# A layernorm-and-adapter kernel on one core: a fourth rotating PSUM bank, two biases folded into the transposed state, the residual fetched again by DMA, and a new order on every engine

## The reference

```
xn = layernorm(x)
# attention branch
q = elu(split(xn @ Wq + bq)) + 1 ;  k = elu(split(xn @ Wk + bk)) + 1 ;  v = split(xn @ Wv + bv)
k = k / sqrt(sum(k*k, per head) + 1e-6)
out = merge((q k^T) v) @ Wo + bo
y = xn + out ;  att = (y - mean(y)) / sqrt(var(y) + 1e-6) * gamma + beta
# feed-forward branch, blk = 0, 1, 2 ; linear_l(a) = a @ dequant(q_l)^T + bias_l + (a @ la_l^T) @ lb_l^T
h = xn
for blk in range(3):
    t = gelu(layernorm(linear_{2 blk}(h)) * ln_gamma[blk] + ln_beta[blk])
    h = linear_{2 blk + 1}(t) + h
result = x + att + h
```

## Time and profile before

| | |
|---|---|
| time, median of 3 runs | 634.25 us (634.12 to 634.41) |
| the profiled execution's own time | 636.37 us |
| its span, first to last instruction | 634.6 us |
| mean granted TensorE clock | 0.983 of 2.4 GHz |
| PE busy | 602.0 us, 95% |
| DVE, ACT, POOL busy | 498.5, 446.8, 414.2 us (79%, 70%, 65%) |
| one body (batches 1 to 6) | 74.8 to 74.9 us |

### The profile page before, as it was taken

The page is one execution under the profiler, slowest core; times in us unless marked ns, Lnnn a source line. Parts: engine busy times, 40 slices in busy tenths (PEclk is TensorE's granted clock), DMA queues, the critical chain, the costliest instruction groups (busy, mean ns, idle before and its releaser), DMA issues.

```text
span 634.6 us, 10275 instructions
## 1 busy us (share of the span) xinstructions
PE 602.0 (95%) x3357; PEld 515.6 (81%) x3357; DVE 498.5 (79%) x1079; ACT 446.8 (70%) x699; POOL 414.2 (65%) x361
## 2 busy tenths in 40 slices
PE   7999999899998999989998999989999899989996
PEld 6888879788887888878787888878888787877875
DVE  2678689787888869788797868887787886978578
ACT  2558876858678586786778776784967857777653
POOL 3766766676476756757477674867667585765664
PEclk9999999899998999989999999989999899999999
DMA  8201001200021000300002000120002000010001
GB/s 239 71 3 34 33 1 41 93 1 2 1 99 33 0 0 0 132 0 0 0 33 99 0 0 0 71 61 0 0 0 106 26 0 0 0 67 1 1 1 67
DMA packets 9442, 20.88 MB, mean 33 GB/s; under 512 B 2367, under 2 KB 4302, under 8 KB 9422
## 3 DMA queue, kind: packets, MB, share of 16 engines
q1 hardware_dynamic: 8944, 20.22, 9.5%
q10 hardware_dynamic: 478, 0.41, 0.2%
HBM read 12.24 MB, written 8.39 MB: 33 GB/s over the span
## 4 chain that ended last, share of the span: by engine, by line
PE 51%; DVE 16%; ACT 12%; POOL 10%; issue 7%; DMA 2%; DVEq 0%; POOLq 0%; ACTq 0%; SPq 0%
PE bank L1427 14%; PE bank L1554 9%; PE bank L1433 7%; PE bank L1565 6%; PE bank L1527 3%; POOL sqs L404 3%; ACT fw L614 2%; POOL XNB L399 2%; DMA out_dram<-RES 2%; DVE Y L1030 2%; PE bank L1606 2%; DVE RES L1036 2%; POOL rsf L368 2%; DVE Y L1010 2%; PE bank L1519 2%
## 5 line engine op out<-in xcount | busy, mean ns | idle before, releaser
L253 POOL TENSOR_TENSOR gl<-fw,gh 128x512 fp32r<-128x512 f32 x80 | 102.6, 1298 | 55.9 <-ACT gh L619 55.8
L404 POOL TENSOR_TENSOR sqs<-fw 128x512 f32<-128x512 f32 x48 | 61.8, 1287 | 51.0 <-ACT fw L604 50.8
L604 ACT ACTIVATE fw<-bank,b1c 128x512 f32<-128x512 f32 x96 | 61.6, 683 | 46.4 <-PE bank L1433 46.2
L614 ACT ACTIVATE fw<-fw,vec 128x512 f32<-128x512 f32 x96 | 74.9, 808 | 9.7 <-DVE fw L935 9.4
L935 DVE SCALAR_TENSOR_TENSOR fw<-bank,b1c,rb 128x512 f32<-128x512 f32 x96 | 68.2, 744 | 10.7 <-ACT rb L610 10.7
L368 POOL TENSOR_TENSOR rsf<-vef,neghalf 128x4 f32<-128x4 f32 x48 | 51.6, 1074 | 33.8 <-DVE vef L928 31.3
L258 POOL TENSOR_TENSOR hTl<-hT,hTh 128x512 fp32r<-128x512 f32 x40 | 57.9, 1468 | 16.4 <-ACT hTh L623 16.3
L1554 PE MATMUL bank<-K,XN 128*128 128x256 f32 x256 | 61.9, 379 | 0.0
L610 ACT ACTIVATE rb<-bank 128x512 f32<-128x512 f32 x48 | 28.6, 595 | 45.3 <-PE bank L1527 45.3
L1598 PE MATMUL bank<-M,qT 128*128 128x256 f32 x256 | 59.4, 379 | 0.0
L368 POOL TENSOR_TENSOR rs<-ve,neghalf 128x2 f32<-128x2 f32 (+1 forms) x48 | 39.7, 835 | 29.9 <-DVE ve L1021 18.5
(11 more groups left out here) (148 smaller groups left out, 1681.1 us busy)
## 6 DMA issues: line engine op xcount, KB each, us to landing
X<-in_L_attn_x_dram SPq DMA_DIRECT2D x16, 512.0 KB, 3.7
out_dram<-RES SPq DMA_DIRECT2D x14, 512.0 KB, 2.6
XNB<-in_L_ffn_qweights_dram SPq DMA_DIRECT2D x2, 512.0 KB, 7.4
out_dram<-RES SPq DMA_DIRECT2D x4, 256.0 KB, 2.1
RES<-in_L_ffn_qweights_dram SPq DMA_DIRECT2D x1, 512.0 KB, 6.3
Y<-in_L_ffn_lora_a_dram ACTq DMA_DIRECT2D x4, 96.0 KB, 7.6
Wp<-in_L_attn_Wq_dram SPq DMA_DIRECT2D x1, 256.0 KB, 4.9
Wp<-in_L_attn_Wk_dram SPq DMA_DIRECT2D x1, 256.0 KB, 5.2
```

The lines of the kernel that those rows point to most:

```text
L253: engine.tensor_tensor(gl[:, h, m, :], fw[:, h, m, :], gh[:, h, m, :].bitcast(F32), ALU.subtract).then_inc(g_low[h][m], 1)
L404: pool.tensor_tensor(sqs[:, h, :], fw[:, h, 0, :], fw[:, h, 1, :], ALU.add).then_inc(sqs_ready[h], 1)
L604: act.activation(fw[:, h, m, :], FB[h][m][:], ACT.Square, bias=b1c[:, m, j:j + 1]).then_inc(sq_ready[h], 1)
L614: act.activation(fw[:, h, m, :], fw[:, h, m, :], ACT.Gelu, bias=lnb[:, m, j:j + 1], scale=lng[:, m, j:j + 1]).then_inc(g_ready[h], 1)
```

## The change

**Banks.** `AB` joins as a fourth rotating bank, but with a list of its own: the uses in `ON_SIDE` take it in turn (`SIDE`), the others rotate over the three (`RING`). G is one of its uses. **Residual.** `RES` is filled by a second DMA of x (`load_res` on SP, after the store of the batch before); `base_x`, `beta_sum` and two broadcast rows go. Beta plus the last bias is added, once for all batches, to the bias of block 1's second linear, so that the state hT carries it from there; what block 2's first linear would make of it is subtracted from its bias (`bias_last`, `shift_sums`, `bias_shift`, once in the head). **Variance.** The row sums stay in the bank and the step that scales them and adds epsilon reads them there. **`base_xn`** works by pairs of tiles: four of 128x512 a batch in place of two of 128x1024. **Orders.** All queues are written in a new order.

```
-                pool.tensor_tensor(RES[:, h * HT:(h + 1) * HT, :], X[:, h * HT:(h + 1) * HT, :],
-                                   beta_r[:].unsqueeze(1).broadcast_to([P, HT, D]), ALU.add).then_inc(x_based, 1)
+            def base_xn(i, p, at):
+                pool.tensor_tensor(XNB[:, 2 * p:2 * p + 2, :], XN[:, 2 * p:2 * p + 2, :],
+                                   bo_r[:].unsqueeze(1).broadcast_to([P, 2, D]), ALU.add).then_inc(xn_based, 1)
...
+            def load_res(i, h, at):
+                    sp.wait_ge(stored[h], 16 * i)
+                sp.dma_start(RES[:, h * HT:(h + 1) * HT, :],
+                             x_rows[bass.ds(i, 1), :, h * HT:(h + 1) * HT, :].rearrange("o p t d -> (o p) t d")
+                             ).then_inc(res_loaded[h], 16)
...
-                sp.wait_ge(x_based, nth(i, 2, h))
+                sp.wait_ge(xn_ready, nth(i, NT, h * HT + HT - 1))
                 load_x(i + 1, h)
...
-                dve.tensor_reduce(vsum[:, h, :], RB[r][:].rearrange("p (t n) -> p t n", t=HT), AX_X, ALU.add
+                dve.tensor_reduce(RB[r][:, 0:HT], RB[r][:].rearrange("p (t n) -> p t n", t=HT), AX_X, ALU.add
-                dve.tensor_scalar(vef[:, h, :], vsum[:, h, :], 1.0 / D, EPS_LN, ALU.mult, ALU.add
+                dve.tensor_scalar(vef[:, h, :], RB[r][:, 0:HT], 1.0 / D, EPS_LN, ALU.mult, ALU.add
...
+ON_SIDE = {("k", 1), ("k", 3), ("rs", 1, 0), ("g",), ("m",), ("out", 1), ("out", 3),
+           ("w", 1), ("w", 3), ("w", 5), ("sumv",), ("xt0", 0, 1)}
+                lists, banks = (SIDE, 1) if use in ON_SIDE else (RING, NROT)
...
# PE, body
                 turn_squares(i, 1, 0, BODY)
+                project_q(i, 0, 1, BODY)
                 spread_rstd(i, 1, 0, BODY)
                 project_q(i, 0, 0, BODY)
-                project_q(i, 0, 1, BODY)
                 project_q(i, 1, 0, BODY)
# ACT, body
                 g_higher(i, 0, 2, 0)
+                ln1_normalise(i + 1, 1, BODY)
+                rb_copy(i, 1, 2, BODY)
                 g_higher(i, 0, 2, 1)
-                rb_copy(i, 1, 2, BODY)
```

More of the change, by code:

```diff
@@ L27 @@
 NEWTON = 3
+NVEC = 2 * NBLK + 2 * NBLK + 1
 HEAD, BODY, TAIL = range(3)
@@ L220, in block_kernel @@
         xT_ready = sem("xT_ready")
-        rot_full = [sem(f"rot_full{n}") for n in range(NROT)]
+        rot_full = [sem(f"rot_full{n}") for n in range(NROT + 1)]
         ffn_full = [[sem(f"ffn_full{h}{m}") for m in range(NC)] for h in range(2)]
@@ L320, in body @@
             def body(i):
+                load_res(i, 0, BODY)
+                load_res(i, 1, BODY)
                 next_x(i, 0)
@@ L326, in tail @@
             def tail(i):
+                load_res(i, 0, TAIL)
+                load_res(i, 1, TAIL)
                 store_pair(i, 0)
@@ L462, in head @@
                 ffn_root(0, 0, 1)
+                ln1_root(1, 0)
                 ffn_root(0, 1, 1)
-                base_x(0, 1, HEAD)
+                base_xn(0, 3, HEAD)
                 g_lower(pool, 0, 0, 1, 1)
-                base_xn(0, 1, HEAD)
                 g_lower(pool, 0, 1, 1, 0)
@@ L1126, in bias_centre, with bias_last, bias_shift @@
                 ins.then_inc(vecs_ready, 1)
+            def bias_last():
+                dve.wait_ge(vecs_ready, 2)
+                dve.tensor_tensor(shift[:], vec[:, :, NVEC - 1], vec[:, :, NL - 1], ALU.add).then_inc(shift_ready, 1)
+                dve.wait_ge(shift_ready, 1)
+                dve.tensor_tensor(vec[:, :, NL - 3], vec[:, :, NL - 3], shift[:], ALU.add).then_inc(shift_ready, 1)
+                dve.tensor_copy(shiftr[:, :, 0], shift[:]).then_inc(shift_split, 1)
+                dve.wait_ge(shift_split, 1)
+                dve.tensor_tensor(shiftr[:, :, 1], shift[:], shiftr[:, :, 0].bitcast(F32), ALU.subtract
+                                  ).then_inc(shift_split, 1)
+            def bias_shift():
+                r, n = rotating(0, ("shift",), HEAD)
+                dve.wait_ge(vecs_ready, 3)
+                dve.wait_ge(rot_full[r], n + 1)
+                for part in range(2):
+                    if part:
+                        dve.wait_ge(shift_out, 1)
+                    dve.tensor_tensor(b1c[:, :, NBLK - 1], b1c[:, :, NBLK - 1],
+                                      RB[r][:, 0:2 * NC].rearrange("p (c two) -> p c two", two=2)[:, :, part],
+                                      ALU.subtract).then_inc(shift_out, 1)
             def bias_first():
@@ L1550, in add_g @@
                     pe.wait_ge(kh_ready, nth(i, NT // 2, t // 2))
-                if t == 0 and at != HEAD:
-                    pe.wait_ge(g_copied, nth(i - 1, 1, 0))
+                if t == 0:
+                    take(i, ("g",), at)
                 for c in range(NC):
@@ L1645, in row_sums, with shift_sums @@
                         ins = pe.matmul(RB[r][:, 2 * m:2 * m + 2], w[:, 0, k, m * P:(m + 1) * P], onesr[:],
+                                        start=(n == 0), stop=(n == len(pairs) - 1))
+                ins.then_inc(rot_full[r], 1)
+            def shift_sums():
+                r = take(0, ("shift",), HEAD)
+                pe.wait_ge(wT_split, NL - 1)
+                pe.wait_ge(shift_split, 2)
+                pairs = [(k, w) for k in range(NC) for w in (WTl, WTh)]
+                for m in range(NC):
+                    for n, (k, w) in enumerate(pairs):
+                        ins = pe.matmul(RB[r][:, 2 * m:2 * m + 2], w[:, NL - 2, k, m * P:(m + 1) * P], shiftr[:, k, :],
                                         start=(n == 0), stop=(n == len(pairs) - 1))
@@ L1869, in tail @@
                 spread_rstd(i, 0, 0, TAIL)
-                project_k(i, 2, TAIL)
                 project_k(i, 3, TAIL)
                 turn_squares(i, 1, 0, TAIL)
+                project_q(i, 0, 0, TAIL)
                 spread_rstd(i, 1, 0, TAIL)
+                second_high(i, 0, 0, TAIL)
+                second_low(i, 0, 0)
+                project_q(i, 1, 0, TAIL)
+                second_high(i, 1, 0, TAIL)
                 project_q(i, 0, 1, TAIL)
-                second_high(i, 0, 0, TAIL)
```

527 lines of the change are left out of this document (264 added, 263 removed), and 27 rows, old and new, of tables (BODY_USES, HEAD_USES, TAIL_USES).

## The result

627.23 us, median of 4 runs (627.18 to 627.6), against 634.18 (633.34 to 634.41) for the kernel before in the same session: a ratio of 0.9894 [0.9877, 0.9911], 7.0 us faster. The forecast was 622.4, 11.8 us faster. The profiled execution took 627.22 us, span 625.5, against 636.37 (span 634.6), so that the two profiles differ by 9.15 us. In a later session the medians were 627.04 us and 636.25, 9.2 us apart: how large the gain comes out depends on which of its times the kernel before shows (see the experiments).

A forecast was written before the change was run, and what follows sets the result against it. PE bounds the kernel, with a stall at spread_rstd and the lower clock behind it costing 3.9 us a body. Bodies 8.4, head 2.2 and tail 1.2 sum to 11.8 us off 634.25: 622.4 us, range 608 to 634.5.

The forecast's parts named there:

- bodies: Six bodies: each gains 1.4 us, 8.4 us in all.
- head: Before body 1: two project_q replace two pairs of fillers; between 0 and -4 us, taken as -2.2.
- tail: After the bodies: same stall, same 1.39 us filling, partly given back; between +1 and -3 us, taken as -1.2.
- The stall: PE at spread_rstd of half 1, block 0: one project_q in front cuts idleness from 2.3 to about 1.0 us.
- Most of that would fall into waits anyway: If the lower clock stayed behind the stall, most of its 1.6 us a body would fall into waits.
- No stall as short as 1.04 us brings the clock down in the tail, and not even the one of 2.18 us does: From the tail's stalls: full clock taken behind the shortened stall in the bodies.
- ACT late next: Second products of block 0: PE waits 0.8 and 0.7 us for copies of g; of 3.0 us, 1.5 are left.
- DVE after that: Residual of half 1 to block 1's variance: 7.8 to 8.35 us for 7.04; gain at spread_rstd taken as 1.2.
- The rest of a body: Block 1's spread_rstd to body's end: no change to squares of block 2; 0.2 us of remaining idleness given the new order.
- Cut loop, added DMA, variance in the bank: base_x off the path once the loop is cut, 1 MB a batch of DMA hidden, bank read taken as nothing.
- The fourth bank: PE's banks: each reader comes before its bank is wanted, closest at spread_rstd of half 1, 14.0 against 15.0.
- Slower rival: ACT's ln1_normalise ahead of the last rb_copy delays the last block, up to 3.3 us a body: 642; chance 0.16.

The follow-up runs named there:

- after_unfill: Changed kernel with project_q (0, 1) put back behind spread_rstd (1, 0) in the body: 631.09 us, against 627.04 for the changed kernel.
- before_cut: Kernel before with RES filled by DMA and no base_x, beta and last bias left out of the sum: 636.14 us, ratio 1.0004 to before.
- before_fill_cut: Kernel before with both project_q (0, 0) moved in front of spread_rstd (1, 0) and RES by DMA without base_x: 638.66 us, ratio 1.005 to before.
- after_end: Changed kernel with before's order behind turn_squares (1, 2) on ACT, POOL, PE and DVE: 632.12 us, against 627.04 for the changed kernel.
- after_vsum: Changed kernel with the variance's row sums in SBUF again: 627.08 us, against 627.04 for the changed kernel.
- before_fill: Kernel before with project_q (0, 0) in front of spread_rstd (1, 0) and project_q (1, 0) behind half 1's second product: 639.01 us, ratio 1.0054 to before.
- after_head2: Changed kernel with Wq loaded behind Wk and the front of before's head on the engines: 624.80 us, against 627.04 for the changed kernel.
- after_split: Changed kernel with ACT's copies of g earlier and DVE's k_rstd cut in three among the residuals: 660.16 us, ratio 1.0394 to before.
- after_gh: Changed kernel with ACT's gelu and g_higher (0, 0, 1) earlier and q_exp behind the copies of g: 635.87 us, against 627.04 for the changed kernel.

## Why the prediction was right and wrong

The direction and the range held; the size was 11.8 us for 7.0. Sum by sum, against the profiled pair: bodies 8.4 forecast, 11.0 measured; head +2.2, measured -2.1; tail +1.2, measured +0.2. That is 9.1 where the sum had 11.8. From 9.1 to the 7.0 of the medians it is 2.1 us more, and these are the profiled execution's own: the sum was made from a profile of the upper group of before's times, with a fall of the clock in every body, and taken off a median of the lower group. That the total missed by no more is in part luck: the bodies gave 2.6 us more than forecast, which covered part of the 4.3 us by which the head came out worse.

- **The stall.** Filled as said: 0.79 us of idleness for 1.0, full clock, `second_high` at 18.3 for 18.2, the copies of g at 20.2 for 20.0, half 1 done at 25.7 for 25.3, `spread_rstd` of block 1 at 35.6 in the range of 35.2 to 35.8.
- **What it is worth: right in size, wrong in cause.** The forecast added 1.4 us of idleness and 1.6 of lower clock to 3.0 and let one half fall into waits, whichever it was. The two are not alike. `after_unfill` shows that the idleness falls into waits whole (73.07 us against 73.05), and that the clock is the gain, 1.1 us a body; the body of `before_cut` at full clock shows it from the other side, 1.4 us. "Most of that would fall into waits anyway" was said of a filled body at the lower clock. No run shows one; in an unfilled body it did not fall into waits.
- **"No stall as short as 1.04 us brings the clock down in the tail, and not even the one of 2.18 us does"** rested on one execution, so that "full clock behind it" was right with some luck. The same stall brought it down in the next profile, and one of that length in the bodies of `after_unfill` did in four and not in two. What holds in both profiles of the changed kernel: with stalls up to 0.87 us it never fell while PE worked. By the Trainium skill's rule of repeated waits ("TensorE: Matmul & The Clock Gate", HAM oscillation) it would fall each time. The page's case has longer waits, for DMA; here the bodies of before follow it, those of `after_unfill` only in part, and those of `before_fill_cut`, with waits of 1.15 and 1.85 us, not at all.
- **ACT late next**: PE waits 0.86 and 0.35 us for it; forecast 0.8 and 0.7.
- **DVE after that.** The first `k_hat` took 0.70 us to the next start; forecast 0.88 to 1.45. The variance began at 32.8; forecast 33.1 to 33.65. `turn_squares` starts at 32.2 and ends as DVE gets there, so that DVE is no longer late alone, and `k_rstd` is DVE's sensitive place, which the forecast did not see.
- **The rest of a body**: "of which I give the new order 0.2" is the mis-sized term. It is worth 0.76 (`after_end`), with the next batch's last transposes between the rows on PE, the root of the next batch's half 1 out of the place in front of POOL's four `g_lower`, and its normalisation earlier on ACT.
- **Cut loop, added DMA, variance in the bank**: nothing, as forecast (`before_cut`, `after_vsum`). After the head no engine waits for X or RES.
- **The fourth bank** was given no worth of its own. What it is worth by itself was not run; without it, with the third `project_q` behind the second product, the filling loses 3 us (`before_fill`).
- **Head.** The wrong sign. The forecast counted two pairs of fillers and did not follow what stands in front of them: `qk_sums` went from 9.8 to 15.2. Putting the front of before's head back returns 2.2 us (`after_head2`).
- **Slower rival**: `rb_copy` at 320.25 still waits for PE, so it never came about.

With 1.1 and 0.76 for the bodies, six times, the experiments give 11.2 us for the 11.0. The parts depend on each other, though. Told from the kernel before, the clock gives 1.4 us (74.86 to 73.45), and all the rest of the change together 0.4 (73.45 to 73.05): the 0.76 at the body's end less what the new order loses in front of it. That rests on the one body of before's order that was seen at full clock. The tail's missing 1.0 us was not tried.

## What to carry to other kernels

A stall can cost more by what it does to the clock behind it than by its idleness: compare bodies of one profile in which the clock fell with those in which it did not before you price the idleness. A step in the chain that ended last may be worth nothing when removed; take it out alone. And a queue written anew in the head must be followed from its first entry, since an early step moved by 5 us can outweigh the fillers saved behind it.

## What the hardware showed that was not expected

- A 128x128 operation on DVE with two SBUF inputs takes 0.29 us alone and 1.27 to 1.37 us beside a 128x512 `tensor_tensor` of POOL, and the next one again. In `after_split` six of them in a body come with a body of 78.6 us in place of 73.0.
- The same stall of 2.2 us, in the same place of the same program, brings the clock to 0.50 in some bodies and executions and not in others. A fall costs 0.8 (`before_fill`) to 1.5 us (`after_gh`) in a body and 0.2 us at most in the tail. The times of the kernel before lie in two groups near 634 and 636.5 us and go with the mean clock, though the one lower execution with a profile had an earlier head besides. Why the clock falls or not stays open.
